# Expert down product with the weights held in the array, later router rounds on values, leftover steps placed by hop

## What is computed

```python
x = x + mixer(layernorm(x))
x = x + cross_attention(layernorm(x), ctx, mask)
# experts, E = 8, FF = 256, K = 2, on the layernormed x:
scores = (einsum('btd,ed->bte', x, router_w) + router_b) / temp
for _ in range(3):                                   # on logs
    scores = scores - logsumexp(scores, axis=-1)     # over the experts
    scores = scores - logsumexp(scores, axis=-2)     # over the tokens
gates = exp(scores); gates = gates / (sum(gates, -1) + 1e-8)
vals, idx = top_k(gates, 2); w = vals / (sum(vals) + 1e-8)
g = relu(einsum('btd,edf->btef', x, wg)); p = einsum('btd,edf->btef', x, wp)
all_out = einsum('btef,efd->bted', g * p, wo)
out = x + sum over the two chosen experts of w * all_out
```

## Time and profile before

| | us |
|---|---|
| median of 3 runs | 431.03 |
| lowest, highest | 424.16, 431.24 |
| the profiled execution | 426.72 |
| its span, first to last instruction | 425.0 |

### The profile page before, as it was taken

How to read it: one execution, slowest core, us unless ns; L and a number is a source line. 1 busy time by engine, 2 the same in 40 slices (tenths; PEclk the granted TensorE clock), 3 DMA queues, 4 the chain that set the end, 5 groups by cost and what they waited for, 6 DMA issues and landing times.

```text
span 425.0 us, 6290 instructions
## 1 busy us (share of the span) xinstructions
PE 364.5 (86%) x2199; PEld 250.2 (59%) x2199; DVE 241.6 (57%) x682; ACT 149.2 (35%) x300; POOL 56.5 (13%) x85
## 2 busy tenths in 40 slices
PE   1465269779997999888998999999999999999996
PEld 0353146453454634554455436888788887888875
DVE  2374538864188653873379622766567555545553
...
DMA packets 17297, 15.39 MB, mean 36 GB/s; under 512 B 4469, under 2 KB 16693, under 8 KB 16981
## 3 DMA queue, kind: packets, MB, share of 16 engines
...
q10 hardware_dynamic: 384, 0.20, 0.2%
...
## 4 chain that ended last, share of the span: by engine, by line
PE 69%; DVE 15%; ACT 5%; DMA 5%; issue 3%; POOL 1%; ACTq 1%; SPq 0%; DVEq 0%; POOLq 0%
PE pS L1059 14%; DVE nmax_mask L911 5%; PE pS L1217 4%; PE pC L1232 4%; PE pS L253 4%; PE pS L255 4%; PE pS L254 4%; PE pC L1229 3%; PE pS L1214 3%; PE pA L253 3%; PE pA L255 3%; PE pA L254 3%; PE pB L253 3%; PE pB L254 3%; PE pB L255 3%
## 5 line engine op out<-in xcount | busy, mean ns | idle before, releaser
L1059 PEld LDWEIGHTS pS<-prob,sig 128*128 128x128 f32 x512 | 64.7, 191 | 13.9 <-DVE res L723 6.3
L712 DVE TENSOR_TENSOR sig<-xi_f,pS 128x512 f32<-128x512 f32 x64 | 43.9, 687 | 49.9 <-PE pS L255 44.9
L1059 PE MATMUL pS<-prob,sig 128*128 128x128 f32 x512 | 69.1, 279 | 1.2 <-DVE sig L712 1.0
L911 DVE TENSOR_REDUCE nmax_mask<-pS 128x3 f32<-128x462 f32 (+1 forms) x96 | 52.3, 575 | 12.4 <-PE pS L1184 12.3
L639 ACT ACTIVATE prob<-pS 128x512 f32<-128x512 f32 x80 | 42.1, 600 | 27.6 <-PE pS L1217 27.6
L723 DVE SCALAR_TENSOR_TENSOR res<-pS,w_gate,res 128x128 f32<-128x128 f32 (+1 forms) x128 | 36.0, 344 | 13.9 <-PE pS L1059 12.5
L556 ACT ACTIVATE xi_f<-pA 128x512 f32<-128x512 f32 x32 | 19.1, 597 | 61.0 <-PE pA L255 60.9
L1181 PE MATMUL pS<-k_stack,q_stack 72*128 72x154 bf16 x256 | 35.7, 245 | 2.0 <-DMA q_stack<-q_scr 1.9
L556 ACT ACTIVATE xi_f<-pB 128x512 f32<-128x512 f32 x32 | 19.1, 597 | 51.3 <-PE pB L255 51.2
L1184 PE MATMUL pS<-mbias,ident_bf 128*128 128x462 bf16 (+1 forms) x96 | 35.2, 367 | 0.0
L1181 PEld LDWEIGHTS pS<-k_stack,q_stack 72*128 72x128 bf16 x256 | 21.5, 105 | 10.1 <-DVE nmax_mask L911 4.1
...
## 6 DMA issues: line engine op xcount, KB each, us to landing
...
```

The costliest lines, as they stand in the source:

```text
L712: dve.tensor_tensor(hid[:, i % 2, :], relu[:, i % 2, :], pUp[i % 2][:, :], ALU.mult).then_inc(s_hid, 1)
L911: dve.tensor_reduce(nmax[:, qt, hs[0]:hs[-1] + 1], score_bank(b, n)[:, 0:len(hs) * KEYS].rearrange("p (h k) -> p h k", k=KEYS), AX.X, ALU. ...
L1059: last = pe.matmul(pO[:, toks], hid[:, i % 2, toks], wo_sb[:, e, hf, :], start=(hf == 0 and t == 0), stop=(hf == HF - 1), skip_group_check ...
```

## The change

1. **Down product.** `wo`, split into a high and a low part (`woP`, in the memory of `q_stack[0]`), is the stationary operand, the hidden tile the moving one: three one-pass matmuls of 128 x 512 per unit. The product stands with features in the partitions, one bank per batch (`pO[b % 2]`), and is summed over all 16 units of a batch there. The gate therefore must be applied before: the gate of an expert for all 512 tokens is spread over the partitions by DMA (`w_scr`, `fetch_gate`, `w_wide`), and DVE's first instruction of a unit takes relu and gate in one (`gated`); the relu on ACT and the four `gated_sum` instructions are gone. The hidden tile is split: ACT makes the high part, POOL the low part (`hid_lo`). At the end of a batch ACT copies the bank, PE transposes it, DVE adds it to `res` (`out_copy`, `out_T`).
2. **Router.** The first round still works on logs over experts; the maximum over tokens is found through a 16-row transpose and is brought back by a matmul with ones. From then on the values themselves are scaled: sums over tokens are matmuls with `all_ones`, sums over experts DVE reductions. Group 0's `gates` move from slots 30 to 34 of row 3 into slots 8 to 12, and a new step `gates_T` (slot 15) transposes the gates and starts the DMAs.
3. **wo.** It is fetched in four pieces and split in row 3 (`load_wo`, `split_wo`), on ACT and POOL, instead of fetched whole at the row's end.
4. **Order.** `down` follows its `up` by two units (`LAG`), all 64 units are in `STEPS`, and `LEFT_AT` places each leftover step after a named unit.

```diff
-        LEFT_STEPS = [1, 1, 3, 2, 3, 3, 3] + SINKHORN_ITERS * [2, 2, 2, 2, 2] + [1, 1, 1, 1]
-        ROUTER_AT = ([34, 35, 36, 37, 38, 39, 40, 41, 42, 44, 45],
-                     [0, 0, 1, 1, 2, 5, 5, 5, 7, 10, 10, 10, 11, 11, 12, 15, 15, 15, 17, 20, 20, 30, 32, 34])
+        WO_AT = ([0, 0, 6, 9], [5, 8, 11, 14])
+        OUT_T_AFTER = 2
+        LEFT_AT = [0, 1, 1, 2, 2, 3, 4, 5, 5, 5, 7, 8, 8, 9, 8,
+                   10, 11, 11, 11, 12, 12, 13, 14, 14, 15, 15, 15, 16, 16, 17, 18, 18, 18, 19, 19, 20, 21, 22, 23]
+        ROUTER_AT = ([34, 35, 35, 36, 37, 38, 39, 40, 41, 42, 42, 43, 44, 45],
+                     [0, 2, 3, 4, 6, 7, 8, 10, 12, 15])
...
+                elif step == "gates_T":
+
+                    sp.wait_ge(s_wrow, b + 1)
+                    sp.dma_start(w_scr[GB * E * b:GB * E * (b + 1), :], w_rows).then_inc(s_wscr, 16)
+                    if b == 0:
+                        sp.wait_ge(s_wscr, 16)
...
+                        for e in range(E):
+                            if e == 4:
+                                sp.wait_ge(s_pv, G * NB)
+                            fetch_gate(0, e)
...
+                elif step == "split_wo":
+
+                    pool.wait_ge(s_wohi, n + 1)
+                    cols = slice(n * WO_COLS, (n + 1) * WO_COLS)
+                    pool.tensor_tensor(woP[1][:, cols], wo_raw[:, n % 2, :], f32(woP[0][:, cols]), ALU.subtract
+                                       ).then_inc(s_wolo, 1)
+                elif step == "expert_up":
+
+                    u = N * b + n
+                    pool.wait_ge(s_hidhi, u + 1)
+                    pool.tensor_tensor(hid_lo[u % NHID], hid[:, u % 2, :], f32(hid_hi[u % NHID]), ALU.subtract
+                                       ).then_inc(s_hidlo, 1)
...
+                    dve.wait_ge(s_gp, u + 1)
+                    dve.wait_ge(s_wide[n // HF], 16 * (b + 1))
...
+                    dve.scalar_tensor_tensor(out=gated[:, u % 2, :], in0=pGate[u % 2][:, :], scalar=0.0,
+                                             in1=w_wide[n // HF], op0=ALU.max, op1=ALU.mult).then_inc(s_gated, 1)
+                    dve.wait_ge(s_gated, u + 1)
+                    dve.wait_ge(s_up, u + 1)
+                    if u >= 2:
+                        dve.wait_ge(s_hidlo, u - 1)
+                    dve.tensor_tensor(hid[:, u % 2, :], gated[:, u % 2, :], pUp[u % 2][:, :], ALU.mult
+                                      ).then_inc(s_hid, 1)
...
-                for t in range(T):
-                    toks = slice(t * P, (t + 1) * P)
-                    last = pe.matmul(pO[:, toks], hid[:, i % 2, toks], wo_sb[:, e, hf, :],
-                                     start=(hf == 0 and t == 0), stop=(hf == HF - 1), skip_group_check=True)
-                last.then_inc(s_down, 1)
...
+                pe.matmul(ps, w_hi, hid_hi[u % NHID], start=(n == 0), stop=False, skip_group_check=True)
+                pe.matmul(ps, w_lo, hid_hi[u % NHID], start=False, stop=False, skip_group_check=True)
+                pe.wait_ge(s_hidlo, u + 1)
+                pe.matmul(ps, w_hi, hid_lo[u % NHID], start=False, stop=(n == N - 1), skip_group_check=True
+                          ).then_inc(s_down, 1)
...
+                elif step == "col_sum":
+
+                    pe.wait_ge(s_gexp, b + 1)
+                    if n > 0:
+                        pe.wait_ge(s_tm, TM_PER * b + 7 + 5 * n)
                     for t in range(T):
...
+                        last = pe.matmul(pSink[b][:, 2 * P:2 * P + GB * E], all_ones[:, :],
+                                         route["gate"][:, b, t, :, :].rearrange("p b e -> p (b e)"), start=(t == 0),
+                                         stop=(t == T - 1), skip_group_check=True)
```

More of the change, by code:

```diff
@@ L173, in build_decoder @@
         mask_sb = nmax_mask[:, 0:T * KEYS].bitcast(I32).rearrange("p (t k) -> p t k", t=T)
-        elog, eexp = mixT[0:GB * E, :], q_f[0:GB * E, :]
-        relu = xi_f
-        hid = sig
+        N = E * HF
+        UNITS = NB * N
+        NHID = 3
+        gated = sig
+        hid = xi_f
+        hid_hi, hid_lo = ([xi[p][:, 0, :], xi[p][:, 1, :], act_in[p][:, :]] for p in range(2))
+        woP = [q_stack[0][:, p * E:(p + 1) * E, :].rearrange("p a n -> p (a n)").bitcast(F32R) for p in range(2)]
+        w_rows = q_f[0:GB * E, :]
+        w_wide = [x1[:, :, :].rearrange("p t d -> p (t d)"), decay[:, :], xn[:, :, :].rearrange("p t d -> p (t d)"),
+                  q_parts[:, 0:2, :].rearrange("p a n -> p (a n)").bitcast(F32)] + [prob[:, i, :] for i in range(4)]
+        out_T = cn
         pT, pA, pB, pS0, pS1, pS2, pC, pG = (bank(n) for n in ("pT", "pA", "pB", "pS0", "pS1", "pS2", "pC", "pG"))
@@ L315, in router @@
         def router(grp):
-            steps = [("logits", grp, 0)]
-            for it in range(SINKHORN_ITERS):
-                steps += [(name, grp, it) for name in
-                          ("expert_max", "expert_exp", "expert_sum", "expert_ln", "expert_log", "to_experts",
-                           "token_max", "token_exp", "token_log", "to_tokens")]
-            return steps + [("gate_exp", grp, 0), ("gates", grp, 0), ("gates", grp, 1), ("gates", grp, 2)]
+            steps = [(name, grp, 0) for name in (
+                "logits", "add_bias", "expert_max", "expert_exp", "expert_sum", "expert_ln", "expert_log", "col_max_T", "col_max",
+                "col_max_back", "col_shift", "col_exp", "col_sum", "col_norm")]
+            for it in range(1, SINKHORN_ITERS):
+                steps += [("row_norm", grp, it), ("col_sum", grp, it), ("col_norm", grp, it)]
+            return steps + [("gates", grp, 0), ("gates", grp, 1), ("gates", grp, 2), ("gates_T", grp, 0)]
         def post(b):
@@ L368, in build_decoder @@
             elif b == NB - 1:
+                place([("load_wo", 0, i) for i in range(WO_STEPS)], WO_AT[0])
+                place([("split_wo", 0, i) for i in range(WO_STEPS)], WO_AT[1])
                 place(router(0)[len(ROUTER_AT[0]):], ROUTER_AT[1])
@@ L374, in build_decoder @@
             STEPS += [step for slot in slots for step in slot]
-        units = [(b, i) for b in range(GB) for i in range(E * HF)]
-        rest = iter(last_group(NB - 1)[1:] + post(NB - 1) + router(1))
-        left = [[next(rest) for _ in range(n)] for n in LEFT_STEPS]
-        STEPS += last_group(NB - 1)[:1] + [("expert_up", *units[0])]
-        for k, unit in enumerate(units):
-            if k + 1 < len(units):
-                STEPS.append(("expert_up", *units[k + 1]))
-            STEPS.append(("expert_down", *unit))
-            STEPS += left.pop(0) if left else []
-        STEPS += [step for steps in left for step in steps]
+        rest = last_group(NB - 1)[1:] + post(NB - 1) + router(1)
+        left = [[step for step, at in zip(rest, LEFT_AT, strict=True) if at == u] for u in range(UNITS + LAG)]
+        STEPS += last_group(NB - 1)[:1]
+        for u in range(UNITS + LAG):
+            if u < UNITS:
+                STEPS.append(("expert_up", *divmod(u, N)))
+            if u >= LAG:
+                STEPS.append(("expert_down", *divmod(u - LAG, N)))
+                if (u - LAG) % N == N - 1:
+                    STEPS.append(("out_copy", (u - LAG) // N, 0))
+            if u >= LAG + OUT_T_AFTER and (u - LAG - OUT_T_AFTER) % N == N - 1:
+                STEPS.append(("out_T", (u - LAG - OUT_T_AFTER) // N, 0))
+            STEPS += left[u]
+        STEPS += [("out_T", NB - 1, 0)]
         block = ctx.enter_context(nc.Block())
@@ L1003, in _ @@
                 elif step == "gates":
                     gates(b, n)
-            dve.wait_ge(s_res, NB)
-            with dve.Fori(GB, NB) as b:
-                for i in range(E * HF):
-                    hidden(b, i)
-                    if i >= HF and i % HF == 0:
-                        gated_sum(b, i // HF - 1)
-                gated_sum(b, E - 1)
         @block.tensor
@@ L1288, in _ @@
+                    last.then_inc(s_gateT, 1)
                 elif step == "expert_up":
@@ L1295, in _ @@
                     if (b, n) == (0, 0):
-                        pe.wait_ge(s_wo, 16)
-                        pe.wait_ge(s_wo2, 16)
+                        pe.wait_ge(s_wolo, WO_STEPS)
                     down(b, n)
-            pe.wait_ge(s_route, ROUTE_STEPS * GROUPS)
-            N = E * HF
-            with pe.Fori(GB, NB) as b:
-                up(b, 0)
-                for i in range(N):
-                    if i + 1 < N:
-                        up(b, i + 1)
-                    down(b, i)
+                elif step == "out_T":
+                    pe.wait_ge(s_outc, b + 1)
+                    transposes(pO[b % 2], lambda t: out_T[:, t, :]).then_inc(s_outT, 1)
 _INS = ["x", "ctx_1024", "mask_1x1xSxS2_if1", "L0_attn_Win", "L0_attn_bin_", "L0_attn_Bp", "L0_attn_Cp", "L0_attn_Dp",
```

310 lines of the change are left out of this document (177 added, 133 removed).

## The result

The changed kernel takes 423.45 us (median of 21 runs, 420.54 to 433.65) against 429.51 before (21 runs, 424.16 to 437.96). The ratio, which leaves disturbed runs out, is 0.9906 with an interval of 0.9878 to 0.9934: 4 us faster, less than half of the 8.5 that I forecast. The time lies in the range, the size of the gain was wrong. There all seven runs of before lie between 430.3 and 432.0; of the 21 here eight are under 428.

What follows compares the result with a forecast made beforehand. The prediction took PE to bound the expert phase and DVE row 3's SA part. Expert phase and end -12.7, row 3 +1.2 + 2.5 and DMA +0.5 gave -8.5 us, from 426.72 to 418, range 410 to 427.

Steps and rivals of the forecast that it cites:

- The unit: Expert phase: nine one-pass matmuls at 0.235 us make a unit 2.115 us, 64 units 135.4; two pO banks remove the 0.45 wait.
- The other engines in a unit: Expert phase, per unit: DVE 1.44 us, POOL 1.27, ACT 0.59, all below PE's pace of 2.115.
- the rival of taking turns: Expert phase: DVE's gated and product also wait for POOL's hid_lo, a unit is 2.71 us, total about 445; chance 0.06.
- slow `down` matmuls: Expert phase: down matmuls take 0.3 us each instead of 0.235, 12 us more, total 430; chance 0.04.
- I take 2 us of PE waiting: First 24 units: DVE's leftover instructions, blocked by POOL, make PE wait 2 us, from 0 to 6.
- 79 of them are 8.8: Expert phase: PE's 79 small leftover matmuls and transposes at 0.112 us each cost 8.8 us; out_T's transposes add 1.3.
- The end: After the last unit: PE waits 1.2 us for the low part; behind PE's end come 4.9 us for 4.0.
- Experts and end together: Expert phase and end: 146.7 + 2 + 4.9 = 153.6 us against 166.3, so -12.7.
- +1.2 + 2.5: Row 3's SA part: DVE's own work grows by net 1.2 us; POOL's four splits block DVE for 2.5, from 0 to 5.1.
- DMA: 0.5 forecast: Row 3, near max_rows: the gate rows' transfers from gates_T delay the chain by 0.5 us, at worst 2.8.
- The first router round in row 2: Row 2: it loses an ACT exponent on 16 x 512 and gains small matmuls, net 0.
- The profiled execution lies between them; I keep 418.: Base of the forecast: profiled execution 426.72 us, between the median 431.03 and the lowest run 424.16; gives 418.2.

Runs made afterwards that it cites:

- after_again: The changed kernel, nothing edited, run again on another chip for a second profile; 422.46 us against 431.32 for the kernel before, ratio 0.978.
- no_hid_lo: Changed kernel without the hidden tile's low part; down's third matmul reads the high part again, so PE's work is the same; 422.81 us.
- moved_all: Changed kernel with group 0's gates and the wo splits in row 3's SB slots, router sums spaced, group 1's gates_T behind unit 27; 422.38 us.
- best: Changed kernel with router steps spaced, group 0's gates and gates_T in row 3's SB, wo splits left in SA, group 1's gates_T behind unit 27; 418.65 us.
- before_again: The kernel before the change, nothing edited, run again for a second profile; 432.29 us.

## Why the prediction was wrong

I compare before (425.0) and after_again (418.5), both without the half clock behind row 2's logits: -6.4 where I said -8.5. Of these, 2.0 are the wait in row 0, which differs as much between two profiles of one kernel; -4.4 is left. That it comes near the 4.0 of the ratio is partly luck, since the medians give 6.1 and one chip 8.9. By stage the -4.4 are -10.9 in the expert phase, +5.9 in row 3, +0.7 in row 2 (0.2 of it the wait for `max_rows`) and -0.1 elsewhere.

The step that failed is the price of what the other engines do to the bound one: row 3 (+3.7 forecast, +5.9 measured) and PE's waits in the first 24 units (2 forecast, 3.5 and 1.6 by the clock measured).

- **The unit: right.** 2.07 for 2.115, 64 of them 2.9 us less than forecast. Both banks of `pO` and the stationary weights do what was said.
- **The other engines in a unit: right.** `gated` and the product 0.69 with POOL's 1.30 beside them, so the rival of taking turns falls, and so do slow `down` matmuls. The Trainium skill, page "SBUF — State Buffer", section "Who interferes with whom", says that a DVE instruction with at most one SBUF input, outside the two-port modes, stays out of the lock on the port pair; the trace agrees on both sides, 0.69 there and 1.30 against 0.22 at L1086, which has two.
- **PE waiting in the first 24 units: too small, and at another place.** "I take 2 us of PE waiting". It waits 0.61 + 0.92 + 1.94 = 3.5, and the last is followed by half clock, 1.6 us more at unit 24 (3.68 for 2.07). That `hid_lo` makes leftover DVE work late was right: without it 0.92 and 1.49 of the 1.94 are gone (no_hid_lo). But I looked for the waits ahead of `gate`, ended by `gated`, and there is none. PE waits where a leftover step of its own needs DVE's result, for `xn_post` at unit 8 and for `w_gate` at unit 23, and the slack of two units is no help there. The 0.61 is for ACT, another cause. That a wait can cost more than its length through the clock was missing.
- **Leftover PE work: too small.** "79 of them are 8.8", and the transposes 1.3. The transposes take 1.3. The others take 10.1: units 1 to 23 less their `up` and `down` matmuls at 0.23 each, the three waits and one `out_T`. Behind a group of small matmuls the second `up` matmul starts 0.31 us after the first instead of 0.23; about a dozen groups pay that, 1 us.
- **The end.** PE waits 0.7 there, not 1.2, and 4.8 us follow for the 4.9 of the forecast (whose own terms, 0.6, 0.6, 0.7, 0.3 and 2.6, add up to 4.8).
- **Experts and end together:** 153.6 - 2.9 + 1.5 + 1.6 + 1.3 - 0.6 = 154.5, measured 155.4. Most of the rest, 0.9, is at the first and the last unit; what it is stays open. Against before that is -10.9, not -12.7.
- **Row 3: the main miss.** "+1.2 + 2.5" against 5.9, or 6.2 in the first profile, whose rows are shown above. The blocks were named rightly and cost 1.30 + 1.23 + 1.17 - 0.62 = 3.1. DVE's own work grew by 2.1, not 1.2: from start to start the four instructions on 16 x 512 had taken 2.5, not 2.8, and the ten small ones, which now stand one behind the other, take 2.2 for 1.6. The third term I had left out: DVE idles 0.53 + 1.16 + 0.26 = 1.95 for PE, where it idled 0.97 before, so +1.0. Together 3.1 + 2.1 + 1.0 = 6.2. The idle pieces of 0.53 and 1.16 stand behind the first `col_sum` of the part, for which PE had waited 0.74, and behind the matmuls on the values that follow it; behind the second wait, 1.21, only 0.26 follows. With the steps spaced 1.2 is left of 1.95 (moved_all, best), so some 0.7 of the idle time is `col_sum`'s.
- **DMA: 0.5 forecast, none found in row 3.** From the maxima's cast to the first SB score 5.5 us in row 3, as before (5.5).
- **The first router round in row 2: "0", measured 0.5** (21.3 and 21.8).
- **The base: not examined.** "The profiled execution lies between them; I keep 418." The runs of both kernels spread over 13 us, and the two stretches of half clock in row 2 are 3 to 5 of them. The profiled execution had none there; before_again, which had both, took 432.29. I had the granted clock of every slice on the page and did not ask why it fell.
